# A routed feed-forward kernel: the shared network of blocks 4 to 7 moved out of the routing front

## The reference

```
h = layernorm(x) * (1 + cb) + sb
n = h * rsqrt(mean(h * h) + 1e-8) * norm_weight
shared = relu(n @ sw1 + sb1) @ sw2 + sb2            # 128 -> 512 -> 128
probs = sigmoid(n @ router_w.T); top 2 of 8 experts, weights w = scores / sum
routed = sum over the two experts of w_e * (relu(n @ ew1[e] + eb1[e]) @ ew2[e] + eb2[e])
out = x + gb * (shared + routed)                     # gb: gate per block and column
```

## Time and profile before

| what | value |
|---|---|
| median of three runs | 1091.35 us (1087.33 to 1092.53) |
| the profiled execution's own time | 1089.98 us |
| its span, first to last instruction | 1088.1 us |
| mean granted clock of TensorE | 0.961 |
| busy: TensorE, VectorE, ScalarE, GpSimd | 87%, 88%, 78%, 71% |
| Mamba steps | up to about 758 us |
| routing front | 758 to 880 us |
| wait for the first tile | 880 to 894 us |
| 23 expert tiles | 894 to 1054 us |
| results written, loaded, added, put out | 1054 to 1088 us |

### The profile page before, as it was taken

One profiled execution on the slowest core, in us unless ns is written; L12 is line 12 of the kernel. 1 busy time (PEld: TensorE's weight loads), 2 busy tenths in 40 slices (PEclk: granted clock), 3 DMA queues, 4 the chain that ended last, 5 costly groups with the idle time before them and its releaser, 6 DMA issues.

```text
span 1088.1 us, 20653 instructions
## 1 busy us (share of the span) xinstructions
PE 948.3 (87%) x6072; PEld 543.3 (50%) x6072; DVE 959.5 (88%) x1769; ACT 846.6 (78%) x1604; POOL 777.4 (71%) x942
## 2 busy tenths in 40 slices
PE   5799999999999999999999999985888759999970
PEld 4344554454445544544554445443455537777750
DVE  6799999999999999999999999975888948888855
ACT  4699999899999998999899989974777625555530
POOL 1289989998998999888877886873355643666660
PEclk9799999999999999999999999998899969999995
DMA  5010232224222322100000000000011136776628
GB/s 151 17 27 13 73 140 71 71 80 152 72 71 85 128 76 86 64 3 3 4 10 2 4 4 4 4 2 1 20 35 35 40 116 190 233 229 224 226 89 231
DMA packets 57422, 83.93 MB, mean 77 GB/s; under 512 B 17562, under 2 KB 37664, under 8 KB 57312
## 3 DMA queue, kind: packets, MB, share of 16 engines
q1 hardware_dynamic: 52320, 74.13, 21.3%
q0 software_dynamic: 4992, 8.48, 2.3%
HBM read 44.99 MB, written 37.83 MB: 76 GB/s over the span
## 4 chain that ended last, share of the span: by engine, by line
PE 28%; ACT 22%; POOL 21%; issue 17%; DVE 8%; DMA 2%; SPq 1%; POOLq 1%; DVEq 0%; ACTq 0%
ACT E L976 3%; POOL dtx L1788 3%; POOL own L1820 3%; PE bank L468 3%; ACT xbc L1081 3%; PE bank L689 2%; POOL yt L1842 2%; PE bank L546 2%; POOL xw L1795 2%; PE bank L703 2%; PE bank L701 2%; PE bank L700 2%; ACT L1070 2%; POOL y L1846 2%; PE bank L690 2%
## 5 line engine op out<-in xcount | busy, mean ns | idle before, releaser
L1449 DVE SCALAR_TENSOR_TENSOR cv<-bank,PAR,cv 128x511 f32<-128x511 f32 (+2 forms) x384 | 276.5, 740 | 6.1 <-ACT cv L988 2.0
L976 ACT ACTIVATE E<-bank 128x512 f32<-128x512 f32 x256 | 144.5, 603 | 44.7 <-PE bank L532 40.1
L1465 DVE SCALAR_TENSOR_TENSOR M<-E,bank 128x512 f32<-128x512 f32 x256 | 170.2, 676 | 1.4 <-ACT E L976 0.4
L1917 POOL DMA_INDIRECT RS<-y,XR x92 | 99.5, 1082 | 78.1 <-DVE y L1697 53.6
L468 PE MATMUL bank<-hn,WA 128*128 128x512 f32 x256 | 142.5, 640 | 3.5 <-DVE cv L1449 3.5
L1842 POOL TENSOR_TENSOR yt<-yt,ti 128x384 f32<-128x384 f32 x64 | 64.1, 1002 | 74.4 <-DVE ti L1522 74.4
L1910 POOL DMA_INDIRECT XS<-stage,IDX x64 | 68.5, 1071 | 56.5 <-DVE run L1424 39.2
L1173 ACT ACTIVATE hr<-bank,W1B 128x512 f32<-128x512 f32 x92 | 63.5, 690 | 56.7 <-PE bank L691 48.9
L1612 DVE TENSOR_TENSOR hL<-hr,hH 128x512 fp32r<-128x512 f32 x124 | 86.9, 701 | 4.3
L1788 POOL TENSOR_TENSOR dtx<-xtok,DTW 128x256 f32<-128x256 f32 x128 | 79.8, 623 | 12.0 <-ACT xtok L996 8.1
L1846 POOL TENSOR_TENSOR y<-yt,zs 128x512 f32<-128x512 f32 x64 | 82.2, 1284 | 5.0
(11 more groups left out here) (239 smaller groups left out, 2586.2 us busy)
## 6 DMA issues: line engine op xcount, KB each, us to landing
XS<-PADT SPq DMA_DIRECT2D x32, 520.0 KB, 4.8
W1B<-WD SPq DMA_DIRECT2D x23, 514.0 KB
W2B<-WD SPq DMA_DIRECT2D x23, 512.5 KB
WD<-WS SPq DMA_DIRECT2D x16, 512.0 KB, 2.9
XR<-XS SPq DMA_DIRECT2D x23, 260.0 KB
RW<-w_in SPq DMA_DIRECT2D x18, 256.0 KB, 4.9
xin<-x_in SPq DMA_DIRECT2D x4, 512.0 KB, 8.5
PC<-p SPq DMA_DIRECT2D x128, 6.0 KB
```

The costliest lines, as they stand in the source:

```text
L976: f(E[i % 2][:, :], bank[2 + i % 2][:, :], ACT.Exp).then_inc(e_a, 1)
L1449: stt(out=cv[t][:, s:L], in0=src[:, 0:L - s], scalar=PAR[:, bass.ds(cw + 3 - s, 1)], in1=cv[t][:, s:L], op0=ALU.mult, op1=ALU.add).then_in ...
L1465: stt(out=M[i % 4][:, :].rearrange("p (n t) -> p n t", n=4), in0=E[i % 2][:, :].rearrange("p (n t) -> p n t", n=4), scalar=1.0, in1=bank[5 ...
L1917: nc.gpsimd.indirect_dma_start(RS[:, :], bass.IndirectOffsetOnAxis(ap=XR[i % XD][:, (c + 1) * ROW - 1:(c + 1) * ROW].bitcast(I32), axis=0) ...
```

## The change

The shared network now has its own place per block. Blocks 0 to 3 (`NSH = 4`) keep it in the front. Blocks 4 and 5 (up to `HEAD = 6`) run it in a new step `gap()` between the front and the first tile. Blocks 6 and 7 run it behind the last tile, as if they were tiles 23 and 24 of `expert(i)`. The norms and the routing of all eight blocks stay in the front as they were.

What goes with it: the normed halves of blocks 4 to 7 have buffers of their own, in the memory that the late `RA` and `RB` use, so the loads of `RA` and `RB` of blocks 4 to 7 wait for the up-projection of their block. The numbers of the projection passes (`q`) follow the new order (`network`). The bases of blocks 4 and 5 are turned in bank 6, the one of block 5 inside the first tile. The gate rows are worked out behind the last tile (`gate_rows`), their VectorE part one column block per tile in tiles 2 to 9 (`gate_column`). The last tile's result is turned inside pass NT+1, behind the first projections of blocks 7 and 6. VectorE's final sum waits for the gate rows once, and per block for its base.

```diff
+NSH = 4
+HEAD = 6
+        def base_bank(n):
+            return bank[6 if NSH <= n < HEAD else 7]
+        def network(n):
+            return n if n < HEAD else NT + n
...
             for b in range(NB):
+                if b >= NSH:
+                    wait(sp, u_mm, HT * (network(b) + 1))
...
@@ tensor: front, the same for relu, keep_base, result (scalar) and add_shared, halves (vector)
-                if 0 <= i - 1 < NB:
+                if 0 <= i - 1 < NSH:
                     turn_base(i - 1)
-                if 0 <= i < NB:
+                if 0 <= i < NSH:
                     shared_up(i, 0)
...
             def expert(i):
-                q = NB + i
+                q = HEAD + i
...
-                        if i == 0 and t < 2:
-                            wait(pe, gb_a, t + 1)
                         up(q, t, W1B[i % 2], nH[:, half], nL[:, half])
-                    if i > 0:
+                    elif i < NT + NB - HEAD:
+                        shared_up(HEAD + i - NT, t)
+                    if 0 < i <= NT:
                         if t == 0:
                             wait(pe, w2_in[(i - 1) % 2], 16 * ((i - 1) // 2 + 1))
                         down(q - 1, t, W2B[(i - 1) % 2])
-                    if t == 0 and i > 1:
+                    elif i > NT:
+                        shared_down(HEAD + i - 1 - NT, t)
+                    if t == 0 and 2 <= i < NT + 2:
                         turn_result(i - 2)
+                    if t == 1 and i == 0:
+                        turn_base(HEAD - 1)
                     if t == 2 and i + 1 < NT:
                         turn_slots(i + 1)
+            def gap():
+                for t in range(HT):
+                    shared_up(NSH, t)
+                for n in range(NSH + 1, HEAD):
+                    for t in range(HT):
+                        shared_up(n, t)
+                        shared_down(n - 1, t)
+                for t in range(HT):
+                    shared_down(HEAD - 1, t)
+                for n in range(NSH, HEAD - 1):
+                    turn_base(n)
+                turn_slots(0)
...
-            wait(pe, r_a, HT * NB)
-            wait(pe, dg_v, NB)
-            for g in range(2):
-                mm(bank[g][:, :], ones_row[:, :], DG[:, g * 512:(g + 1) * 512], start=True, stop=True).then_inc(gb_mm, 1)
-            turn_slots(0)
-            for i in range(NT + 1):
+            gap()
+            for i in range(NT + 2):
                 expert(i)
-            turn_result(NT - 1)
+            gate_rows()
+            turn_base(HEAD)
+            expert(NT + 2)
+            turn_base(HEAD + 1)
...
@@ vector
+            def gap():
+                for t in range(HT):
+                    halves(NSH, t)
+                map_tiles()
+                for n in range(NSH + 1, HEAD):
+                    for t in range(HT):
+                        halves(n, t)
+                    add_shared(n - 1)
+                add_shared(HEAD - 1)
+                low_slots(0)
...
-            map_tiles()
-            gates()
-            low_slots(0)
-            for i in range(NT + 1):
+            gap()
+            for i in range(NT + 3):
                 expert(i)
-            weigh(NT - 1)
+            wait(dve, gb_a, 2)
             for b in range(NB):
...
+                wait(dve, base_a, b + 1)
                 tt(RA[b][:, :], RA[b][:, :], h[:, b * L:(b + 1) * L], ALU.add).then_inc(fin_o, 1)
```

More of the change, by code:

```diff
@@ L172, in build @@
         DG, gbB = sb("DG", NB * DM), sb("gbB", NB * DM)
[L173 to L174 removed]
+        RA = [sb(f"RA{b}", L) for b in range(NSH)]
+        RB = [sb(f"RB{b}", L) for b in range(NSH)]
+        scope[0] = ExitStack()
+        nH_late = [sb(f"nH_late{n}", L, F32R) for n in range(NSH, NB)]
+        nL_late = [sb(f"nL_late{n}", L, F32R) for n in range(NSH, NB)]
+        scope[0].close()
+        scope[0] = ctx
+        RA += [sb(f"RA{b}", L) for b in range(NSH, NB)]
+        RB += [sb(f"RB{b}", L) for b in range(NSH, NB)]
         def first_bank(n):
@@ L1249, in expert, with gate_rows @@
                         relu(q, t, W1B[i % 2][:, 2 * HE + t:2 * HE + t + 1].bitcast(F32))
+                    elif i < NT + NB - HEAD:
+                        shared_relu(HEAD + i - NT, t)
+                    if t == 1 and i == 0:
+                        keep_base(HEAD - 1)
                     if t == 2 and i + 1 < NT:
                         high_slots(i + 1)
-                if i > 0:
+                if 0 < i <= NT:
                     result(q - 1, W2B[(i - 1) % 2][:, 2 * HE:2 * HE + 1].bitcast(F32))
+                elif i > NT:
+                    shared_result(HEAD + i - 1 - NT)
+            def gap():
+                for t in range(HT):
+                    shared_relu(NSH, t)
+                for n in range(NSH + 1, HEAD):
+                    for t in range(HT):
+                        shared_relu(n, t)
+                    shared_result(n - 1)
+                shared_result(HEAD - 1)
+                for n in range(NSH, HEAD - 1):
+                    keep_base(n)
+                high_slots(0)
+            def gate_rows():
+                for g in range(2):
+                    wait(act, gb_mm, g + 1)
+                    f(gbB[:, g * 512:(g + 1) * 512], bank[g][:, :], ACT.Copy).then_inc(gb_a, 1)
             early_tap(0)
@@ L1259, in _ @@
                 front(i)
-            for g in range(2):
-                wait(act, gb_mm, g + 1)
-                f(gbB[:, g * 512:(g + 1) * 512], bank[g][:, :], ACT.Copy).then_inc(gb_a, 1)
-            high_slots(0)
-            for i in range(NT + 1):
+            gap()
+            for i in range(NT + 2):
                 expert(i)
+            gate_rows()
+            keep_base(HEAD)
+            expert(NT + 2)
+            keep_base(HEAD + 1)
         @block.vector
@@ L1616, in add_shared @@
                 xb = xT[:, n * L:(n + 1) * L]
-                wait(dve, es_a, n + 1)
+                wait(dve, es_a, network(n) + 1)
                 stt(out=xb, in0=es[:, :], scalar=MOD[:, 40 + n:41 + n], in1=xb, op0=ALU.mult, op1=ALU.add).then_inc(fo_v, 1)
@@ L1700, in expert, with gap @@
             def expert(i):
-                q = NB + i
+                q = HEAD + i
                 for t in range(HT):
-                    if i < NT:
+                    if i < NT + NB - HEAD:
                         halves(q, t)
-                    if t == 0 and i > 1:
+                    if t == 0 and 2 <= i < NT + 2:
                         weigh(i - 2)
+                    if t == 1 and 2 <= i < 2 + NB:
+                        gate_column(i - 2)
                     if t == 2 and i + 1 < NT:
                         low_slots(i + 1)
+                if i > NT:
+                    add_shared(HEAD + i - 1 - NT)
+            def gap():
+                for t in range(HT):
+                    halves(NSH, t)
+                map_tiles()
+                for n in range(NSH + 1, HEAD):
+                    for t in range(HT):
+                        halves(n, t)
+                    add_shared(n - 1)
+                add_shared(HEAD - 1)
+                low_slots(0)
             steps(dve, body)
```

107 lines of the change are left out of this document (62 added, 45 removed).

## The result

The changed kernel took 1095.11 us, median of 9 runs (1089.88 to 1096.17), against 1091.35 before: ratio 1.0047, 95% interval 1.0027 to 1.0067. It is slower, though by little. Twelve more runs of it on another chip gave 1094.28 against 1090.87, ratio 1.0040 (1.0020 to 1.0061). The profiled execution of the first set was its fastest, 1089.88, with a span of 1087.4.

A forecast was written before the change was run, and what follows sets the result against it. POOL's scatter issues, not VectorE, were taken to release the first tile, with holes before it and in the tail. Front -2.7, hole 0, first tile +0.7, tail +1.5 gave -0.5 us: 1090.7 us, range 1086.2 to 1095.

The forecast's parts named there:

- the forecast's own 1089 to 1092.5: Whole kernel: the time band of the main forecast itself, without its rivals, given a chance of 0.48.
- a slowing by more than 0.5%: Whole kernel: slower by over 0.5% (5.5 us), needing the upper bounds of tile and tail together; chance 0.07.
- Networks 4 and 5 in the hole: Between front and first tile: networks ready near 883, first rows at 888.1, so hidden with some 5 us to spare, cost 0.
- Front: Routing front: POOL's last issue ends 3.6 us earlier without the moved networks, less 0.9 for TensorE's clock: gain 2.7 us.
- my lower bound: Front's gain of only 1.2 us, with all at half clock and VectorE slightly late from block 5 to 6.
- the 1 us that I had named: Front: forecast wrong if POOL still waits over 1 us for slots before block 6 or 7.
- The half clock that I priced at 0.9: Front, block 4 to 5: two matmul pairs at 1.2 GHz cost 1.9 us, of which half, 0.9, was taken.
- first tile: First tile: turning block 5's base inside it, four transposes and a copy, costs +0.7 us; bounds 0 and 1.5.
- The sign that I had named: Hole: forecast wrong if the networks end after the first tile's rows have landed.
- rival 4: Hole: networks 4 and 5 not hidden, ending 5 us later than worked out; about +1.5 in all, 1092.9; chance 0.05.
- Tail: Behind the last up-projection: tile 22's scatters come +1.1 later and issues take 0.4 more: +1.5 us; bounds 0 and 3.0.

The follow-up runs named there:

- r2: Kernel before with all eight shared networks in the front, only gate columns and gate rows moved behind the last tile: 1091.16 us, ratio 1.0003.
- r10: Kernel before with 24 matmuls without readers in TensorE's idle time between front and first tile: 1090.69 us, ratio 0.9991.
- r1: The changed kernel unaltered, run again on another chip: 1094.28 us against 1090.87, ratio 1.0040.
- r9: The changed kernel with 24 matmuls without readers per block added in the front, blocks 4 to 7: 1088.74 us, ratio 0.9984.
- r11: The changed kernel with 24 matmuls without readers per block in the front (blocks 4 to 7) and 16 in the hole: 1085.56 us, ratio 0.9951.
- r17: The changed kernel with 24 matmuls without readers per block in the front, repeated on another chip: 1093.65 us, ratio 1.0029.
- r18: The changed kernel with 24 matmuls without readers per block in the front and 16 in the hole, repeated on another chip: 1096.93 us, ratio 1.0058.
- r8: The changed kernel with four more POOL scatters behind the 64: 1089.36 us, one run.
- r13: The changed kernel unaltered, run a third time for its profile on another chip: 1095.46 us, one run.
- r14: The changed kernel with four more POOL scatters behind the 64, repeated on another chip: median 1097.32 us, ratio 1.0051.
- r5: The changed kernel with block 5's network down-projection, result and add moved under the first tile's up-projection: 1094.39 us, ratio 1.0034.
- r6: Against the changed kernel: six networks in the front, blocks 6 and 7 in the hole, last down-projection under the first tile, none behind the last: 1094.35 us, ratio 1.0034.
- r7: The changed kernel with TensorE starting the hole's two networks only when all 64 row scatters have landed: 1102.39 us, one run.

## Why the prediction was wrong

Predicted -0.5 us, 1090.7; measured 1095.11, above the range's end of 1095.0 and above the forecast's own 1089 to 1092.5. On a slowing by more than 0.5% I had put 0.07; the measured 0.47% is just short of it. The step that failed is "Networks 4 and 5 in the hole": "Hidden, with some 5 us to spare", at a cost of 0.

- **Front, predicted -2.7.** Measured -2.9, -1.2 and -2.7 in three profiles, of which the second is my lower bound. Against one profile of before this is right; with r2 and r10 as further profiles of an unchanged front the gain would be up to 2.2 us larger. From block 4 to 5 it was 13.9 instead of 14.7 us in the first and 15.1 in r1; POOL still waited 3.39 us before block 5 and 1.71 before block 6, over the 1 us that I had named, so it didn't set the pace there as I had said; that the size came out is in part luck, for in the first profile blocks 5 and 6 gave 0.7 and 1.2 us, where I had counted 1.2 and 0.4. The half clock that I priced at 0.9 was worth more: with TensorE kept busy the front gave 3.8 to 6.5 (r9, r11, r17, r18). I read the removed matmuls as pure relief. They were also what held the clock.
- **Hole, predicted 0, and first tile, predicted +0.7.** Measured by A: +2.4, +3.5 and +2.5. Where the reports came in time (r8, one profile) it was +1.0, so the working of both steps holds there. What failed is the assumption under it, that a hand-over from TensorE to ScalarE costs what it costs elsewhere in the trace. At its worst it was 9.6 to 13.2 us late in each of nine profiles. The 5 us of cover were gone, and everything queued behind the late network (the tile map in r17, the first tile's transposes in all) waited with it. The sign that I had named is there: block 5's result starts at 889.71, when the first tile's rows have long landed (885.6). This is my rival 4 ("they would have to end 5 us later than worked out"), to which I gave 0.05 because I saw no mechanism; its size, +1.5 in all, was also too small.
- **Tail, predicted +1.5.** Measured from tile 22's matmuls to the first load: +1.5 in all three. The first add waits for the rows' DMA and not for network 7, as said. Network 7's add ends at 1066.21, and the final sum's first add starts at 1067.11: 0.9 us to spare.
- **Not in the sum.** First load to end grew by 0.4 to 0.6 with the tail's loads spaced a little wider. In r13 the tile loop took 2.5 us more; I have one such profile and no cause.

Sum of the first profile: -2.9 + 2.4 + 0.0 + 1.5 + 0.6 = +1.6; of r1: -1.2 + 3.5 + 0.0 + 1.5 + 0.5 = +4.3. Predicted: -2.7 + 0.7 + 1.5 = -0.5. r13 comes to +4.2 as well, and the two sets of times say +3.8 and +3.4.

Shown, in the profiled executions: the hole is where the forecast broke, and late reports are what delays it there; A of one kernel grows by 5.8 to 13.5 us with them (r8 and r14, r9 and r17, r11 and r18). The kernel of r9 stands 2.1 us under its before with prompt reports in the profile, and 3.8 above (r17) with late ones; that of r11 5.3 under, and 7.1 above (r18), each at nearly the same clock. Neither the clock nor the tail alone makes the loss. Not shown: what holds the reports, how often they are late in the executions whose traces weren't kept, and whether it is the chip, the execution or the taking of the record that decides. r14's and r18's times fall into two groups on one chip; the groups with late reports are those with an incomplete record; no run separates the three. The changed kernel itself never ran in the groups with prompt reports, and r5 and r6, which did, are 3.9 us over their before all the same, with stages that sum to +2.6 and +2.1. So late reports aren't shown to be all of the loss. Of 0.5 us or more they appear only from the end of the front on (in r2 one of 1.6, in block 7's network), when TensorE runs the networks' matmuls in a row beside POOL's last scatters; in the tile loop, which is as dense and has scatters too, none is over 0.4 us. r7 ran where no report was late in any kernel, so the part of the scatters is open. The Trainium skill (Perfetto Trace Analysis, Tensor Engine Instruction) says that the end of a matmul in a profile is estimated, while the semaphore is updated once PSUM has acknowledged the write. So a recorded end doesn't prove by itself that the work is done; here the six updates within 0.26 us do. The Trainium skill (NOTIFIC — the notification-queue block, Interfaces) names pressure from the record queues as something that can stall an engine; no run here shows such a stall, and the incomplete records are only a hint that way.

No version beat the kernel before on every chip. r11's 0.9951 and r9's 0.9984 didn't stand their repetition (1.0058 and 1.0029).

## What to carry to other kernels

A hole in one engine's timeline is not free cover for work that hands over between three engines: price each hand-over, and above all look what of the awaited path is queued behind the moved work on every engine. Here the tile map and the first tile's transposes were, so a delay that had nothing to do with them went straight to the end. Of putting the moved work behind them, r5 tried the part of the last down-projection, which cost as much at the first tile as it was to save; the tile map ahead of the moved halves in VectorE's order wasn't tried. And repeat a promising run on another chip before believing its interval: a ratio of 0.9951 with an interval clear of 1 turned into 1.0058.

## What was not expected of the hardware

- The latest report of TensorE's matmuls reached ScalarE 9.6 to 13.2 us behind the recorded end in each of the nine profiles with networks in the hole from four groups of runs, and none was late in the six from two others (r5 to r8, r9 and r11). The semaphore's own updates are recorded late too, six of them within 0.26 us. r9 and r17 have the same instructions.
- Taking 24 matmuls per block out of the front lowered the mean granted clock of 758 to 880 us from 0.94 to 0.84 and 0.79, and the mean of a block costs 2.08 instead of 1.12 us at the lower level. 24 matmuls without readers brought 0.93 to 0.96 back; 12 brought 0.90.
